# State space layer: VectorE's order inside a slot (decays of the next tile behind the gate, output sums after them, convolutions last), and TensorE's square sums ahead of a projection

## What is computed

```python
z, xBC, dt = split(u @ W_in.T)                 # 512 gate, 768 convolved, 8 step sizes
xBC = silu(conv_b + sum(shift(xBC, k) * conv_w[:, k] for k in range(4)))
x, B, C = split(xBC)                           # 128, 128, 512 channels
dt = softplus(dt + dt_bias); A = -exp(A_log)
L = exp(segsum(dt * A))                        # decays between two tokens of a sequence, lower triangle
y = ((C @ B.T) * L * dt) @ x + D * x           # 8 heads
y = y * silu(z)                                # the gate
y = y * rsqrt(mean(y * y over 128 channels) + eps) * norm_weight
x_next = layernorm(u + y @ W_out.T)
```

## Time and profile before

| | us |
|---|---|
| three runs | 1164.1, 1167.17, 1168.81 |
| their median | 1167.17 |
| the profiled execution, own time | 1169.61 |
| its span | 1167.7 |
| first `mix` (slot 0) | starts at 627.44 of the span |
| first `queries` of cross attention (slot 16) | starts at 768.88 |

### The profile page before, as it was taken

How to read it: one execution, slowest core, us unless ns; L and a number is a source line. 1 busy time by engine, 2 the same in 40 slices (tenths; PEclk the granted TensorE clock), 3 DMA queues, 4 the chain that set the end, 5 groups by cost and what they waited for, 6 DMA issues and landing times.

```text
span 1167.7 us, 20743 instructions
## 1 busy us (share of the span) xinstructions
PE 1080.9 (93%) x7208; PEld 652.5 (56%) x7208; DVE 788.3 (68%) x1500; ACT 585.7 (50%) x1212; POOL 491.4 (42%) x868
## 2 busy tenths in 40 slices
PE   6899999999999899999978999889998999999997
PEld 3666675555555345777533455567775435545455
DVE  4999978888887242333586687687997565554655
ACT  2666638777778421333286555367874232121210
POOL 6999854666665255333325254472331000000001
PEclk9999999999999899999989999999999999999999
DMA  6965365665563313453503000120000000000000
GB/s 231 315 193 180 107 188 156 149 155 147 152 152 80 95 68 100 130 173 100 168 4 135 1 1 1 37 82 22 9 24 6 1 0 1 13 5 10 9 10 28
DMA packets 82460, 100.36 MB, mean 86 GB/s; under 512 B 13716, under 2 KB 69166, under 8 KB 81678
## 3 DMA queue, kind: packets, MB, share of 16 engines
q1 hardware_dynamic: 74915, 85.97, 25.8%
q0 software_dynamic: 3408, 9.34, 2.3%
q10 hardware_dynamic: 4034, 3.72, 0.9%
HBM read 59.83 MB, written 33.36 MB: 80 GB/s over the span
## 4 chain that ended last, share of the span: by engine, by line
PE 35%; DVE 5%; ACT 5%; issue 4%; POOL 1%; POOLq 0%; ACTq 0%; DVEq 0%
PE cps_h L3102 6%; PE cps_h L2242 3%; PE cps_h L3121 3%; PE cps_x L3135 2%; PE cps_t L2307 2%; PE cps_h L2733 2%; PE cps_x L3160 2%; PE cps_o L3160 2%; PE cps_t L3121 1%; PE cps_o L3121 1%; ACT e_kbd L2548 1%; PE cps_t L3135 1%; PE cps_x L2664 1%; PE cps_o L2688 1%; PE cps_x L2261 1%
## 5 line engine op out<-in xcount | busy, mean ns | idle before, releaser
L2864 POOL TENSOR_SCALAR f_rstd<-f_mv 128x1 f32<-128x1 f32 x16 | 3.8, 239 | 253.0 <-DVE f_mv L3016 252.9
L932 DVE TENSOR_REDUCE b_nm<-a_s 128x4 f32<-128x1024 f32 x64 | 78.1, 1220 | 33.4 <-PE a_s L1049 32.1
L2961 DVE TENSOR_TENSOR f_prod<-f_sg,f_kept 128x512 f32<-128x512 f32 (+1 forms) x48 | 33.2, 692 | 94.8 <-ACT f_kept L2892 90.9
L996 ACT ACTIVATE a_late<-a_qkv 128x512 f32<-128x512 f32 x128 | 76.3, 596 | 40.0 <-PE a_qkv L1109 39.4
L3102 PE MATMUL cps_h<-residT,w_f_w 128*128 128x512 f32 x176 | 80.8, 598 | 3.4 <-DVE f_inner L2998 1.9
L932 DVE TENSOR_REDUCE b_nm<-a_pt 128x4 f32<-128x1024 f32 x64 | 77.0, 1203 | 2.0 <-PE a_pt L1049 2.0
L996 ACT ACTIVATE a_late<-a_y 128x512 f32<-128x512 f32 x128 | 76.4, 597 | 1.9
L2886 ACT ACTIVATE f_sg<-cps_h 128x512 f32<-128x512 f32 (+1 forms) x24 | 14.3, 596 | 123.6 <-PE cps_h L3121 107.6
L1124 PE MATMUL a_o<-a_late,b_vt 128*32 128x256 f32 x1024 | 68.4, 385 | 5.7 <-ACT a_late L996 5.7
L1441 POOL DMA_INDIRECT routed<-c_out,c_target x39 | 37.4, 959 | 68.8 <-ACT c_out L1523 68.5
L2113 DVE SCALAR_TENSOR_TENSOR d_acc<-d_pad,d_cw,d_acc 128x512 f32<-128x512 f32 x72 | 58.0, 810 | 2.8 <-ACT d_acc L2016 1.1
(11 more groups left out here) (448 smaller groups left out, 2906.4 us busy)
## 6 DMA issues: line engine op xcount, KB each, us to landing
kparts<-a_rest SPq DMA_DIRECT2D x48, 192.0 KB, 3.3
a_rest<-a_rest SPq DMA_DIRECT2D x64, 128.0 KB, 3.0
xrows<-in_c_fill SPq DMA_DIRECT2D x13, 387.0 KB, 4.5
c_xrow<-xrows SPq DMA_DIRECT2D x39, 129.0 KB, 2.1
c_back<-routed SPq DMA_DIRECT2D x16, 256.0 KB, 3.3
a_front<-kparts SPq DMA_DIRECT2D x12, 288.0 KB
a_front<-qparts SPq DMA_DIRECT2D x36, 96.0 KB
qparts<-b_xp SPq DMA_DIRECT2D x48, 64.0 KB, 2.9
```

Of the source, the lines that this page charges most:

```text
L932: dve.tensor_reduce(nm[s % 2][:, 4 * n:4 * n + 4].rearrange("p (g h) -> p g h", h=2), s1[step % 2][:], AX.X, ALU.max, negate=True).then_in ...
L996: act.activation(pr[g % 8][:], s2[g % 2][:], ACT.Exp, scale=SCALE).then_inc(s2_out, 1)
```

## The change

Three things move, and nothing is added or removed. On VectorE, in each slot, `time(s + 1)` goes from the end to directly behind `gated(s)`; `weigh` is done for the next tile in this slot (`weigh(s + 1)`) instead of at the start of the next one, behind `mean_square(s - 1)`; `add_up(s - 3)` goes from ahead of `gated(s)` to behind `weigh(s + 1)`; and both convolutions are last. On TensorE `square_sums(s - 1)` goes ahead of the slot's second job.

```diff
             time(0)
+            weigh(0)
             for s in range(SLOTS):
                 if s == TILES:
                     then(dve, -1, 0)
                 todo = later_convolved(s)
                 if live(s):
-                    weigh(s)
+                    gated(s)
+                if live(s + 1):
+                    time(s + 1)
+                if live(s - 1):
+                    mean_square(s - 1)
+                if live(s + 1):
+                    weigh(s + 1)
                 if live(s - 3):
                     add_up(s - 3)
-                if live(s):
-                    gated(s)
-                if live(s - 3):
                     statistics(s - 3)
-                for n in todo[:1]:
+                for n in todo:
                     convolve(n)
-                if live(s - 1):
-                    mean_square(s - 1)
-                for n in todo[1:]:
-                    convolve(n)
-                if live(s + 1):
-                    time(s + 1)
                 if s >= TILES:
                     then(dve, s - TILES, 1)
...
                 if live(s + 1):
                     products(s + 1)
+                if live(s - 1):
+                    square_sums(s - 1)
                 for n in todo[1:2]:
                     fill(n)
                 for q in batch[2:3]:
                     segments(q)
-                if live(s - 1):
-                    square_sums(s - 1)
                 if live(s - 2):
                     put_out(s - 2)
```

## The result

| | before | changed |
|---|---|---|
| runs beside each other (4 each), median | 1167.99 us | 1201.94 us |
| their spread | 1164.1 to 1174.62 | 1200.98 to 1205.63 |
| profiled execution, own time | 1169.61 | 1201.63 |
| first `mix` to first `queries` ("the stretch") | 627.44 to 768.88: 141.44 | 621.46 to 796.87: 175.41 |

The changed kernel is slower: ratio 1.0272, 95% interval 1.0227 to 1.0318. Forecast was 1188 us with a range of 1180 to 1200, so the sign was right and the size too small: the time lies 1.9 us above the range, and far above the likeliest case of 1183 to 1192. Set against the median of 1167.17 from which the forecast was counted, the ratio gives 1198.9 us, just inside the range. The stretch grew by 34.0 us where the forecast had it grow by 18.4 (its new waits of slots 3 to 15, 21.9, less 2.9 and 0.6).

A forecast was written before the change was run, and what follows sets the result against it. TensorE was taken to set the pace where there are jobs, taking turns with VectorE in the last slots. New waits of 23.6 us less 2.9 gained made +20.7, forecast as 1188 us against the median, range 1180 to 1200.

The forecast's parts named there:

- likeliest case: New waits of `put_out` less the gain from earlier `weigh`: 1188 us, within 1183 to 1192, chance 0.60.
- new waits of slots 3 to 15: TensorE waits at `put_out` for the later sums in these slots: 21.9 us.
- `weigh` ahead, gain 2.9: Four TensorE waits for `weigh` in the state space part disappear: 2.9 us gained, the most possible.
- Order of the chain, start of `put_out` at +4.29 to +4.39: With sums behind gate, `time`, `mean_square` and `weigh`, `put_out` can start 4.29 to 4.39 us after `products(s + 1)` starts.
- The 14 places: Slots 3 to 16, where `put_out` was to wait for the sums, some 23 us in all.
- Convolutions last: Two convolutions of 2.32 us end each slot; the gate is at most about 0.3 late in slots 5 and 9, covered.
- ScalarE, which I feared for the same edit: Rival: later activations delay ScalarE's evacuations in nine slots with convolutions, +10 us, 1198 us; chance 0.07.
- The granted clock: Rival: TensorE's clock falls in the new gaps, up to +12 us, 1200 us; chance 0.22.
- the seven places: Slots 6, 10 and 11 to 15, with new gaps of 1.7 to 2.9 us; each could cost 1.8 us more.
- Slot 16 and cross attention, +2.3: `mean_square(15)` ahead of `add_up(13)` makes `put_out(14)` wait 2.3 us; the rest of cross attention keeps its length.
- two rivals: Clock falling in the new gaps, 1200 us, chance 0.22; convolutions holding ScalarE up, 1198 us, chance 0.07.

The follow-up runs named there:

- e5: Changed kernel with GpSimd's two products cut to 1 of 64 columns from tile 4 on (output differs): 1204.76 us, ratio 1.0288 to the kernel before.
- e1: Changed kernel with `add_up(s - 3)` put back ahead of `gated(s)`, all else as changed: 1185.8 us, ratio 1.0000 to the kernel before.
- e3: Changed kernel with extra, unused matmuls on TensorE in the gaps of slots 6, 10 and 12 to 15: 1214.03 us, ratio 1.0247 to the kernel before.
- e2: Kernel before with only `add_up(s - 3)` moved, to directly behind `gated(s)`: 1205.3 us, ratio 1.0157 to the kernel before.
- e6: Changed kernel with the sums ahead of the gate again and slot 6's transpose of x one job later: 1169.06 us, ratio 0.9987 to the kernel before.
- e7: Kernel before with only `square_sums(s - 1)` moved ahead of the slot's second job: 1172.25 us, ratio 0.9998 to the kernel before.
- e9: Changed kernel with the sums ahead of the gate from slot 12 on only: 1189.09 us, ratio 1.0151 to the kernel before.
- e8: Changed kernel with `square_sums` behind the slot's second job as before: 1228.29 us, ratio 1.05 to the kernel before.
- e4: Changed kernel with four buffers instead of two for the norm factors `rs`: 1219.44 us, ratio 1.0287 to the kernel before.
- r_changed: The changed kernel run once more, unaltered, on another chip: 1206.47 us, ratio 1.0301 to the kernel before.

## Why the prediction was off

Step by step, with the length of the stretch slot by slot (mix to mix) in both kernels:

- *`weigh` ahead, gain 2.9:* right as a mechanism. No `mix` waits for it; slot 1 comes 1.90 us sooner. In the slots with a new gap the gain is only part of the difference.
- *Order of the chain, start of `put_out` at +4.29 to +4.39:* right to 0.05 in the last slots: in slot 12 it is 764.73 less 760.29, 4.44, against 4.39. In the slots with jobs I had `square_sums` last 0.95; it takes 1.05 in slots 1 to 15, and slot 5 has 4.45 against 4.29 (680.84 less 676.39). The 14 places are the ones named.
- *Convolutions last, "the next gate can be about 0.3 us late, which the wait for the square sums covers":* **this step failed, by 3.0 us.** I took 2.32 us for a convolution from a place where no product of GpSimd ran beside it, and put what the two engines cost each other at nothing, without a reason. GpSimd's norm steps wait for the sums, and its products stand behind them. Now that the sums come in the middle of the slot, the products run beside the convolutions that follow. They slow the convolutions (e5), and the gate starts 0.98 behind `products` in slot 4 (665.73 less 664.75) where I had 0.17; slots 6, 8 and 10 are late in the same way. ScalarE, which I feared for the same edit, was not held up (e1).
- *The granted clock:* **this is the failed term that matters, 11.3 us (e3).** The mechanism stood in the text with the seven places and "up to +12 us", but as a rival at 0.22 and not in the sum. What I set against it, that `mix` ran at the high level behind a gap of 1.83 in slot 1, was one gap of 1.83 with full work on both sides. The longest new ones are 2.81 and 3.03, and ahead of them stands one-column work; whether that work matters was not tested, and in e2 a fall followed a gap behind full projections (2.47 in slot 6). Six of the eight longest gaps show a fall, slots 11 and 16 none in this execution; in e5 and e3 these two had one. So the rival's 1200 us came close while a likeliest case without it could not. The loop that the page "TensorE: Matmul & The Clock Gate" of the Trainium skill describes under HAM oscillation waits for DMA, some 3 to 5 us at each step. Nearly all the gaps here are shorter, so "every one of these gaps", as I had put it, does not follow from that loop, and two of the eight had no fall.
- *Slot 16 and cross attention, +2.3:* `put_out(14)` waits 2.24 as forecast. From the first `queries` to the end the profiled execution took 402.93 against 398.82, 4.1 more. The other 1.8 have no cause shown. They stand as well in e1, e6, e7 and e9, where `put_out(14)` waits for nothing and this part takes 400.5 to 400.8, so the one profile of before may be a quick one here.

The sum, then, for the stretch: 18.4 forecast, 11.3 of clock, 3.0 of convolutions slowed by products (the waits that e5 took away: 4 places by 0.71 to 0.78), and 1.3 for the 0.16 by which the chain was counted short in each of the eight slots 3 to 10. That makes 34.0, the measured growth. The 1.3 is worked out, not tried, and the fit to the tenth is partly luck, since with filler slot 11 takes 0.4 us more (e3). The profiled execution was 6.0 us faster ahead of the first `mix`, where nothing is changed (621.46 against 627.44), which is why its total is only 32.1 us over that of before. That part differs by as much between kernels that do not change it: 619.84 in e8 and 626.28 in e5, on one chip. And that the measured time lies as near as 2 us to the end of the range is no merit of the sum: the range reached to 1200 for the sake of two rivals.

On convolutions and products running at once, the page "SBUF — State Buffer" of the Trainium skill, Who interferes with whom, says that a VectorE instruction with two inputs in SBUF and a GpSimd instruction that reads SBUF get in each other's way. The traces agree: six convolution instructions took 6.04 us beside the products and 4.54 without them, and the two instructions for the decays (L1922) 2.49 beside convolutions where they took 2.04 apart from them. The slowdown is not the same each time: in slot 5 the one product beside the convolutions kept its 1.04, and they took 5.38.

## What to carry to other kernels

Before a step is moved later, look for the engine that waits for its result through a single buffer: here, with one pair of PSUM banks, sums that came later in the slot made a wait in each of 14 slots, and moving only the other steps had none of that loss (e1). No run gave `put_out` a second pair of banks, so what that would save is not shown. A gap on TensorE costs more than its length if it lets the clock fall: where gaps of 1.2 to 3 us repeat, as here, put the work behind them at half speed into the upper bound at least, and fill a gap to find out. When a step's place shifts in time, price what will now run beside it on the engine that shares the memory, not only what it waits for.

## What the runs showed of the hardware

- Whether the clock falls behind a gap is not settled by the gap's length alone. Behind 1.23 us it fell once and held once in one execution (e2). Behind the 1.78 us that all kernels have ahead of slot 12 it held in before, changed, e1, e3, e4 and e9 and fell in r_changed, e2, e5, e6, e7 and e8, so it differs between executions of one kernel (changed and r_changed). Behind 1.84 and 1.85 it fell in e5 and held in changed; behind 2.24 and 2.25 in slot 16 it held in changed and fell in e3; behind 2.47 and 2.48 it fell once and held once (e2); behind 2.81 it held in slot 9 of e8. In changed, r_changed, e4 and e5 the slots 6, 10, 12, 13, 14 and 15, with gaps of 2.24 to 3.04, all have a fall. What tells the others apart stays open.
- A fall costs more than its own step. Behind a gap of 2.81 us the projection took up to 3.78, and the transpose and the `mix` behind it were at half speed as well (1.06 and 1.15 against 0.60 and 0.68), so that slots 13 and 14 took 11.12 and 9.88 us where with filler they took 7.85 and 7.42.
- Extra matmuls in six gaps made the stretch 10.9 us shorter, although they did nothing but keep the engine busy; 4.0 us of that were lost again behind the first `queries` (e3).
